# A graph network's last attention layer: half of its first products issued ahead of five late transposes

## What is computed

```python
def gat_layer(x, W, a_src, a_dst, bias, src, dst, heads, out_c, concat):
    n = x.shape[0]
    h = (x @ W).reshape(n, heads, out_c)
    al_s = jnp.einsum('nhc,hc->nh', h, a_src)
    al_d = jnp.einsum('nhc,hc->nh', h, a_dst)
    e = jax.nn.leaky_relu(al_s[src] + al_d[dst], NEG_SLOPE)
    m = jax.ops.segment_max(e, dst, num_segments=n)
    ex = jnp.exp(e - m[dst])
    z = jax.ops.segment_sum(ex, dst, num_segments=n)
    alpha = ex / (z[dst] + 1e-16)
    msg = h[src] * alpha[:, :, None]
    out = jax.ops.segment_sum(msg, dst, num_segments=n)
    out = out.reshape(n, heads * out_c) if concat else out.mean(axis=1)
    return out + bias
...
h = gat_layer(x, W1, a_src1, a_dst1, b1, src, dst, heads=8, out_c=96, concat=True)
h = jax.nn.elu(h)
out = gat_layer(h, W2, a_src2, a_dst2, b2, src, dst, heads=1, out_c=768, concat=False)
```

## Time and profile before

| | |
|---|---|
| median of 3 runs | 1476.71 us |
| lowest and highest | 1476.68, 1478.66 us |
| profiled execution: span from its first to its last instruction | 1478.3 us |
| TensorE, matmuls | 1385.0 us busy, 94% of the span |
| TensorE on the chain that ended last | 76% |
| VectorE / ScalarE / GpSimd busy | 771.6 / 445.6 / 547.0 us |
| mean granted TensorE clock | 0.970 |

### The profile page before, as it was taken

One profiled execution on the slowest core, in us unless ns is written; L12 is line 12 of the kernel. 1 busy time (PEld: TensorE's weight loads), 2 busy tenths in 40 slices (PEclk: granted clock), 3 DMA queues, 4 the chain that ended last, 5 costly groups with the idle time before them and its releaser, 6 DMA issues.

```text
span 1478.3 us, 22402 instructions
## 1 busy us (share of the span) xinstructions
PE 1385.0 (94%) x7674; PEld 1283.9 (87%) x7674; DVE 771.6 (52%) x1843; ACT 445.6 (30%) x953; POOL 547.0 (37%) x626
## 2 busy tenths in 40 slices
PE   5999999999999999999999899889998999878797
PEld 3677999999999999999999899879888987777784
DVE  7876755234444365662223444645464615599544
ACT  2555421101100011100100311244574334557631
POOL 8001344242425243343434242034334454436630
PEclk9999999999999999999999999999999999967799
DMA  3111111122344142341212121122102211200001
GB/s 114 54 29 37 33 41 56 33 60 69 97 128 117 40 141 66 104 129 53 65 32 65 53 61 37 39 81 69 41 23 62 88 43 38 75 1 1 1 11 53
DMA packets 57782, 86.47 MB, mean 58 GB/s; under 512 B 6447, under 2 KB 54438, under 8 KB 57563
## 3 DMA queue, kind: packets, MB, share of 16 engines
q1 hardware_dynamic: 45184, 65.82, 15.2%
q10 hardware_dynamic: 12504, 19.36, 4.4%
HBM read 83.24 MB, written 1.92 MB: 58 GB/s over the span
## 4 chain that ended last, share of the span: by engine, by line
PE 76%; DVE 11%; ACT 4%; POOL 4%; issue 3%; DMA 2%; DVEq 0%; ACTq 0%; SPq 0%; POOLq 0%
PE psum L2448 13%; PE psum L2452 13%; PE psum L2451 13%; PE psum L2465 8%; PE psum L2468 8%; PE psum L2926 4%; PE psum L2588 2%; DVE max_scratch L2153 2%; PE psum L2513 2%; POOL w_lo L911 2%; PE psum L2827 1%; PE psum L2976 1%; PE psum L2831 1%; PE psum L2832 1%; PE psum L2437 1%
## 5 line engine op out<-in xcount | busy, mean ns | idle before, releaser
L2448 PE MATMUL psum<-w_lo,xT_hi 128*125 128x384 f32 (+5 forms) x1140 | 389.6, 342 | 7.2 <-DVE x_nat L1879 2.3
L2451 PE MATMUL psum<-w_hi,xT_lo 128*125 128x384 f32 (+5 forms) x1140 | 385.0, 338 | 0.0
L2452 PE MATMUL psum<-w_hi,xT_hi 128*125 128x384 f32 (+5 forms) x1140 | 384.9, 338 | 0.0
L898 POOL CAST w_hi<-w_raw 128x384 fp32r<-128x384 f32 x190 | 104.5, 550 | 590.2 <-PE psum L2452 482.6
L2448 PEld LDWEIGHTS psum<-w_lo,xT_hi 128*125 128x125 f32 (+1 forms) x1140 | 213.0, 187 | 10.7 <-POOL w_lo L911 3.4
L1083 ACT ACTIVATE h_hi<-psum 125x384 fp32r<-125x384 f32 (+1 forms) x120 | 59.1, 492 | 532.2 <-PE psum L2452 527.8
L1721 DVE TENSOR_TENSOR h_lo<-psum,h_hi 125x384 fp32r<-125x384 f32 (+1 forms) x120 | 66.9, 558 | 285.8 <-ACT h_hi L1083 284.5
L2451 PEld LDWEIGHTS psum<-w_hi,xT_lo 128*125 128x125 f32 (+1 forms) x1140 | 213.3, 187 | 0.4
L2452 PEld LDWEIGHTS psum<-w_hi,xT_hi 128*125 128x125 f32 (+1 forms) x1140 | 212.9, 187 | 0.0
L900 POOL TENSOR_TENSOR w_lo<-w_raw,w_hi 128x384 fp32r<-128x384 f32 x190 | 200.9, 1058 | 15.2
L2465 PE MATMUL psum<-h_lo,adjacency 125*125 125x384 f32 (+3 forms) x600 | 203.6, 339 | 2.3 <-issue 1.9
(11 more groups left out here) (348 smaller groups left out, 2220.9 us busy)
## 6 DMA issues: line engine op xcount, KB each, us to landing
w_raw<-weights_dram SPq DMA_DIRECT2D x296, 192.0 KB, 2.4
score_w_raw<-weights_dram ACTq DMA_DIRECT2D x58, 192.0 KB, 2.7
x_nat<-x_dram SPq DMA_DIRECT2D x1, 1875.0 KB
x_residual<-x_dram SPq DMA_DIRECT2D x1, 1875.0 KB
score_a_rows<-L_gnn_a_src_dram ACTq DMA_DIRECT2D x8, 192.0 KB, 3.6
score_a_rows<-L_gnn_a_dst_dram ACTq DMA_DIRECT2D x8, 192.0 KB, 5.0
out_dram<-x_residual SPq DMA_DIRECT2D x4, 375.0 KB
rgcn_bias<-rgcn_bias_dram SPq DMA_DIRECT2D x1, 1125.0 KB
```

The lines of the kernel that those rows point to most:

```text
L898: nc.gpsimd.tensor_copy(mem.wh[:, slot, :], mem.raw[:, raw_slot, :]).then_inc(w_hi_ready, 1)
L2448: ins = nc.tensor.matmul(o, h, wl, start=(j == 0), stop=False, skip_group_check=True)
L2451: nc.tensor.matmul(o, l, wh, start=False, stop=False, skip_group_check=True)
L2452: ins = nc.tensor.matmul(o, h, wh, start=False, stop=stop and j == k - 1, skip_group_check=True)
```

## The change

The second half of the products, and the way the blocks' banks are given out. The first three chunks of all five blocks are issued directly behind `sum_head(7)`, ahead of turns 5 to 9; what is left of each block, chunks 3 to 5, keeps its place between the turns. Five accumulations are so open at once. The banks of the five blocks go from 0, 1, 2, 3, 4 to 0, 2, 3, 4, 1: bank 1 holds head 7's sums, and is now block 4's. Block 4's first half waits for `last_biased`, which VectorE gives at L2356, when it has read that bank.

```diff
-            self.banks = ([1, 2, 0, 3, 4] if heads > 1 else list(range(NB))) + [b % 8 for b in range(NB, NB * n)]
+            self.banks = ([1, 2, 0, 3, 4] if heads > 1 else [0, 2, 3, 4, 1]) + [b % 8 for b in range(NB, NB * n)]
...
-            def q3_begin(m):
-                first_piece(Q3, mem.xh, mem.xl, T_Q[3], m)
-
-            in_steps((lambda m: turn_x3(NB + m), 0), (q3_begin, 2))
+            def q3_half(i, m):
+
+                width = HW + 2 * Q3.heads
+                o = bank(Q3.banks[m], 0, width)
+                pe.wait_ge(xT_lo_ready, T_Q[3] + i * NB + m + 1)
+                if i == 0 and m == 0:
+                    pe.wait_ge(wa_ready, Q3.index + 1)
+                    pe.wait_ge(part_read, Q2.unit0 + LAST)
+                if i == 0 and m == NB - 1:
+                    pe.wait_ge(last_biased, 1)
+                for j in range(i * (KC // 2), (i + 1) * (KC // 2)):
+                    if m == 0:
+                        pe.wait_ge(w_lo_ready, Q3.chunk + j + 1)
+                    slot = (Q3.chunk + j) % WRING
+                    h, l = mem.xh[:, j, nodes(m)], mem.xl[:, j, nodes(m)]
+                    wh, wl = mem.wh_pads[:, slot, 0:width], mem.wl_pads[:, slot, 0:width]
+                    nc.tensor.matmul(o, h, wl, start=(j == 0), stop=False, skip_group_check=True)
+                    nc.tensor.matmul(o, l, wh, start=False, stop=False, skip_group_check=True)
+                    ins = nc.tensor.matmul(o, h, wh, start=False, stop=(j == KC - 1), skip_group_check=True)
+                    if m == NB - 1 and j < KC - 1:
+                        ins.then_inc(w_used, 1)
+                if i:
+                    ins.then_inc(gemm_done, 1)
+                    owed[0] = m == NB - 1
+
+            for m in range(NB):
+                q3_half(0, m)
+            in_steps((lambda m: turn_x3(NB + m), 0), (lambda m: q3_half(1, m), 2))
             chunks_and_scores(Q3, mem.xh, mem.xl)
```

## The result

| | before | changed |
|---|---|---|
| median | 1476.71 us (7 launches, 1471.74 to 1478.99) | 1467.78 us (7 launches, 1464.49 to 1471.41) |
| ratio, 95% interval | | 0.9938 [0.9924, 0.9951] |
| span of the profiled execution | 1478.3 us | 1465.9 us |
| granted clock, mean | 0.970 | 0.975 |

By the ratio the changed kernel is 9.2 us faster (7.2 to 11.2 by the interval) where I forecast 6.5; the medians differ by 8.9. The time, 1467.8, lies 0.9 us under the range. Six further launches, against other launches of before, gave 0.9941 [0.9928, 0.9954]. So the side was right, and the size was too small by more than a quarter.

The account below looks back on a forecast made before the run. TensorE was taken as the bound, with a 5.28 us hole waiting for GpSimd; 6.29 us gained up to the second piece, 6.5 in all, so 1476.71 - 6.5 = 1470.2 us, range 1468.7 to 1472.4.

Parts of the forecast that it names:

- What bounds: From head 7 to the end: TensorE carries the stretch, except a 5.28 us hole before turn 5, waiting for GpSimd.
- The moved products run at full clock, with no wait for block 4: Behind head 7's sums: 45 products at 0.177 us, 7.97 us in all; block 4's condition met 4.1 us early.
- It comes 2.70 us later than before: Turn 5, behind the 45 moved products, starts at 1399.90 instead of 1397.20.
- The span against the median: Whole kernel: profiled span 1.6 us above the median; the 6.5 us gain inside the span was moved over unchanged.
- The slow start, 0.62: First four products behind turn 5, at half clock before: 1.34 us where full speed is 0.71, so 0.62 gained.
- my 1.02: Clock gain around turn 5: 0.40 us up to the first second-half product and 0.62 in the products behind it.
- Turn 5 to the first second-half product, 1.64: From turn 5 to the first remaining product: 1.64 us at full clock, against 2.04 before.
- From there to the second piece, 8.67: From the first second-half product to the second piece: 8.67 us left of 17.26, so that piece starts at 1410.21.
- Behind the second piece: From the second piece to the al_parts transposes: VectorE's L2130 and L2131 wait beside shorter GpSimd splits; gain 6.5 to 7.1.
- The sum: Whole change: 6.29 us gained up to the second piece, 6.5 us at the al_parts transposes and at the end.
- VectorE caught behind long operations: Rival, at L2131 or the score steps: VectorE waits for a long GpSimd L1031; gain only 4.0 to 5.5 us; chance 0.15.
- Half clock: Rival: the 45 moved products run at 0.335 us each, giving 1477.9 to 1485.0 us; chance 0.03.

Follow-up runs that it names:

- late_gpsimd_before: Kernel before plus three added GpSimd additions ahead of the last L1015 and L1018 of head 6; ratio 1.0025 to the kernel before.
- same_again: Kernel before, with no edit, run against itself; ratio 0.9997, launches from 1473.59 to 1479.49 us.
- hole_filled: Kernel before plus 34 products that nobody uses behind head 7's sums, nothing moved; ratio 0.9989 to the kernel before.
- late_gpsimd_change: Changed kernel plus three added GpSimd additions ahead of the last L1015 and L1018 of head 6; ratio 0.9968 to the kernel before.
- two_blocks: Changed kernel, but with the first halves of only blocks 0 and 1 moved ahead of the turns; ratio 0.9982 to the kernel before.
- late_pe_change: Changed kernel plus 13 transposes that nobody uses ahead of head 7's sums; ratio 0.9946 to the kernel before.

## Where the prediction was right, and which step failed

The mechanism held. The time fell 0.9 us below the range because terms of the sum had the wrong size, one above all.

- *What bounds.* Right. GpSimd set turn 5 (late_gpsimd_before), TensorE carries the rest, and what was won ahead of the second piece reached the end: from al_parts to the end of the span it is 58.8 to 58.9 us in three launches of before and 59.1 in two of the changed kernel.
- *The moved products run at full clock, with no wait for block 4.* Right: 8.0 us for 45, clock 1.00.
- *"It comes 2.70 us later than before."* **This is the step that failed**, in its size. It is the difference between the end of the 45 products and GpSimd's end, 7.97 less the hole of 5.28, and the hole was that of one launch. There the 50 sums ahead of turns 0 to 4 had taken 9.9 us (1374.20 to 1384.12, granted clock 0.53), against 8.8 in the changed kernel's profile (1370.01 to 1378.79), and the late sums started 1.5 us later against GpSimd than in any launch without added work; beside VectorE's L2356, L1015 had also taken 2.22 instead of the usual 1.81. Measured against L1009, turn 5 comes 8.63 to 8.85 less 7.37, so 1.3 to 1.5 later: 1.2 to 1.4 us more gained.
- *The span against the median.* I set the profiled span, 1478.3, beside the median time and found it 1.6 above. They aren't the same measure: in every launch that has both, the time is 1.8 to 2.0 us longer than the span. By that the launch took about 1480.2 us (an estimate from those runs), 3.5 above the median and above all seven launches of before. It was a slow one, and the page alone, which gives the span only, didn't tell me.
- *The slow start, 0.62.* Right in kind, and again the size of that one launch. In same_again the first seven products took 2.3 us for 1.24, so 1.1; hole_filled puts the clock, with the turns' part, at 0.9 to 1.3, and my 1.02 is inside.
- *Turn 5 to the first second-half product, 1.64.* Measured 1.65. *From there to the second piece, 8.67.* Measured 8.72.
- *Behind the second piece.* I gave 0.2 for what the VectorE steps would save and named 0.8 as the other end. It was the other end: 2.88 before (1416.50 to 1419.38), 2.09 now. L2130 began 0.15 us ahead of the end of GpSimd's first split and ended 0.05 behind it, and L2131 ended with the second split. So 0.6 more. The rule of the Trainium skill, SBUF — State Buffer, section "SBUF: two separate sides", holds again: L2131 ends 0.03 us after GpSimd's split, L2162 with the end of an L1031.
- *The sum.* In the terms of the forecast: 7.97 - 1.4 + 0.4 + 0.6 to 1.1 + 0.8 = 8.4 to 8.9, measured 8.7 by profile. Inside the first pair of profiles, the same stretch gained 7.2.
- *The rivals.* VectorE caught behind long operations did not happen at al_parts; at `row_parts` it did, L2162 for 1.74 us, and cost 0.2 us: L2170 ended at 1417.29, and the products ahead of the `row_parts` transposes would have let them start at 1417.17 instead of 1417.34. Half clock did not happen. What I gave for it, 0.50 "at every restart behind a hole of 5 us", was too wide: a hole of 5.43 ahead of 1296.49 agrees, but behind holes of 7.58 and 8.40 in the first 20 us of the same profile the clock is given as 1.00.
- *The range.* It was built on the uncertainty of the steps, with 1 us for scatter below. The hole's own spread from launch to launch was not in it.

Still open is why TensorE was at half clock for so long in just that launch. The loop's clock goes up and down in every launch (in stretches of 20 us from 1290 to 1370 it is 0.57, 0.80, 0.84, 0.68 in the first launch, 0.66, 0.83, 0.69, 0.84 in same_again), and the profiles don't say what decides when.

## What to carry to other kernels

A hole is the distance between two engines that run at their own pace, and one profile shows it for one launch. Before a sum is built on it, look whether the waiting engine was at its usual pace ahead of it (here: the granted clock was 0.53 in the 10 us of head 6's sums, and the launch was slower than the median by about 3.5 us), and measure the other engine's end from that engine's own last step. Work that is ready can be moved into such a hole past its end: what goes over it delays the waiting step, but leaves the stretch behind it. And once the hole is full, the lateness that it used to swallow counts.

## What the runs showed of the hardware

Idle time of TensorE of 3.13 and 3.21 us was followed by half clock (late_gpsimd_change, two_blocks), 0.27 to 0.61 us was not. The half clock came late: during the idle time the clock was still 1.00, in the nine transposes right behind it 1.00 and 0.82, and only behind those 0.50. The nine transposes and the 0.52 us wait behind them left the clock at 1.00 in the changed kernel. So did 28 transposes within 4.3 us, with 0.98 us of idle time between them, in late_pe_change. Waste can pay: 34 products that nobody uses, in a hole of 6.4 us, shortened the stretch behind it by 0.9 to 1.3 us in the profile, which the ratio, 0.9989 [0.9977, 1.0002], can neither confirm nor exclude.
